# Causal mask of a cross attention: four products on TensorE, or a select on GpSimd

## What is computed

```
scores = jnp.einsum('bhqd,bhkd->bhqk', qh, kh) * inv_sqrt_d
causal = jnp.tril(jnp.ones((sq, sk), dtype=bool))
scores = jnp.where(causal, scores, jnp.finfo(scores.dtype).min)
attn = jax.nn.softmax(scores, axis=-1)
out = jnp.einsum('bhqk,bhkd->bhqd', attn, vh)
```

## Time and profile before

| | us |
|---|---|
| median of three runs | 1243.26 (1242.33 to 1248.41) |
| the profiled execution | 1251.86 |
| its span, first to last instruction | 1250.0 |

### The profile page before, as it was taken

One profiled execution on the slowest core, in us unless ns is written; L12 is line 12 of the kernel. 1 busy time (PEld: TensorE's weight loads), 2 busy tenths in 40 slices (PEclk: granted clock), 3 DMA queues, 4 the chain that ended last, 5 costly groups with the idle time before them and its releaser, 6 DMA issues. The chain is left out here.

```text
span 1250.0 us, 20961 instructions
## 1 busy us (share of the span) xinstructions
PE 1156.1 (92%) x7761; PEld 911.6 (73%) x7762; DVE 812.8 (65%) x1392; ACT 593.8 (48%) x1402; POOL 370.6 (30%) x279
## 2 busy tenths in 40 slices
PE   7989999999999999999999874899989999999992
PEld 3456677767776777677767653888779988889992
DVE  1155698789878988898889754532266666655660
ACT  1234554465445554555456422411156666656661
POOL 0011102212221222121212111401226566665662
PEclk9989999999999999999999895899989999989997
DMA  7910000000000000000000008202569999999964
GB/s 267 244 72 2 1 9 9 15 14 8 9 15 14 8 9 15 14 8 9 15 14 8 10 14 219 67 27 63 181 210 274 267 271 268 272 264 246 267 116 59
DMA packets 70459, 121.10 MB, mean 97 GB/s; under 512 B 18502, under 2 KB 22134, under 8 KB 70250
## 3 DMA queue, kind: packets, MB, share of 16 engines
q1 hardware_dynamic: 52682, 82.46, 20.4%
q0 software_dynamic: 17728, 37.97, 14.6%
HBM read 93.55 MB, written 28.13 MB: 97 GB/s over the span
## 5 line engine op out<-in xcount | busy, mean ns | idle before, releaser
L1323 POOL TENSOR_TENSOR rall<-qkv_var,phalf 100x17 f32<-100x17 f32 x16 | 49.2, 3074 | 415.4 <-DVE qkv_var L1046 415.4
L1389 POOL DMA_INDIRECT out_rows<-work,idx x64 | 127.9, 1998 | 113.4 <-issue 87.2
L375 PE MATMUL QS<-xh,wh 128*128 128x256 f32 x512 | 148.6, 290 | 0.0
L376 PE MATMUL QS<-xl,wh 128*128 128x256 f32 x512 | 146.0, 285 | 0.0
L377 PE MATMUL QS<-xh,wl 128*128 128x256 f32 x512 | 145.9, 285 | 0.0
L375 PE MATMUL W<-wch,oth 128*100 128x512 f32 x256 | 104.9, 410 | 0.0
L376 PE MATMUL W<-wcl,oth 128*100 128x512 f32 x256 | 100.7, 393 | 0.0
L377 PE MATMUL W<-wch,otl 128*100 128x512 f32 x256 | 100.4, 392 | 0.0
L376 PEld LDWEIGHTS QS<-xl,wh 128*128 128x128 f32 x512 | 99.4, 194 | 1.2
L375 PEld LDWEIGHTS QS<-xh,wh 128*128 128x128 f32 x512 | 99.4, 194 | 1.2
L377 PEld LDWEIGHTS QS<-xh,wl 128*128 128x128 f32 x512 | 99.2, 194 | 0.0
(11 more groups left out here) (206 smaller groups left out, 2874.8 us busy)
## 6 DMA issues: line engine op xcount, KB each, us to landing
raw<-in_w SPq DMA_DIRECT2D x24, 1024.0 KB
raw<-in_w SPq DMA_DIRECT2D x24, 512.0 KB
work<-in_w SPq DMA_DIRECT2D x8, 1024.0 KB
work<-in_w SPq DMA_DIRECT2D x8, 512.0 KB
hx_rows<-h3x SPq DMA_DIRECT2D x16, 212.5 KB
h_columns<-h3s SPq DMA_DIRECT2D x16, 200.0 KB, 1.9
h3T<-h_columns SPq DMA_DIRECT2D x16, 200.0 KB, 4.7
out_rows<-ytiles POOLq DMA_DIRECT2D x16, 200.0 KB, 2.5
```

The costliest lines, as they stand in the source:

```text
L375: mm(dst, ah, bh, start=start, stop=False)
L376: mm(dst, ah, bl, start=False, stop=False)
L1323: return nc.gpsimd.tensor_tensor(out=dst, in0=src, in1=phalf[:, 0:src.shape[1]], op=ALU.pow)
L1389: nc.gpsimd.indirect_dma_start(out, on_rows(idx[:, NE * j + e:NE * j + e + 1]), Y[e % 2][:, 512 * j:512 * (j + 1)], None, compute_op=ALU.a ...
```

## The change

The four products of line 490 are left out, and the first product of each bank in line 496 now opens the accumulation. ACT copies the unmasked scores to `PX` as before and raises `s.sx`. POOL then fills in the mask: one `affine_select` over the 16 heads of `PX`, in place, keeps an element where the query's number (the partition) less the key's number is 0 or more and writes -1e30 elsewhere, and raises `s.sx` a second time. It stands in POOL's queue between `ln1` and `qk`, behind a wait for ACT's copy. PE's queries wait for the copy alone; DVE's maximum in line 1106 waits for the select.

```diff
                     pe.wait_ge(s.ck, b)
-                    for j in range(4):
-                        mm(qb[j][0:T, 0:QW], identb[:, :], mask4[:, :], start=True, stop=False)
                     pe.wait_ge(s.qp, b)
                     for i in range(4):
                         for j in range(4):
 
                             r = slice(DX * j, DX * (j + 1))
                             last = mm(qb[j][0:T, T * i:T * (i + 1)], qpT[r, T * i:T * (i + 1)],
-                                      ckT[r, T * i:T * (i + 1)], start=False, stop=i == 3)
+                                      ckT[r, T * i:T * (i + 1)], start=i == 0, stop=True,
+                                      skip_group_check=True)
                     last.then_inc(s.sx_ps, 1)
...
                     if do.X:
-                        pe.wait_ge(s.sx, b)
+                        pe.wait_ge(s.sx, 2 * b - 1)
                     queries(b + 1)
...
                 if do.X:
-                    dve.wait_ge(s.sx, b)
+                    dve.wait_ge(s.sx, 2 * b)
                     red(mxx[:, :], X3, AX.X, ALU.max).then_inc(s.sx_max, 1)
...
                 if do.Q:
                     ln1(b + 1)
+                if do.X:
+
+                    wait_alone(pool, s.sx, 2 * b - 1)
+                    nc.gpsimd.affine_select(out=PX[0:T, :].rearrange("t (h n) -> t h n", n=T),
+                                            in_=PX[0:T, :].rearrange("t (h n) -> t h n", n=T), pattern=[[0, NX], [-1, T]],
+                                            compare_op=ALU.is_ge, fill=NEG, base=0, channel_multiplier=1).then_inc(s.sx, 1)
+                if do.Q:
                     qk(b + 1)
```

## The result

| | before | after |
|---|---|---|
| median of the runs | 1242.80 us (4 runs) | 1261.68 us (4 runs) |
| ratio, 95% interval | | 1.0158 (1.0084 to 1.0231) |
| profiled execution, its span | 1251.86, 1250.0 | 1268.49, 1266.2 |
| one step of the pipeline | 41.40 | 42.41 |
| last addition of line 1189 (b = 16) starts at | 766.95 | 783.82 |

The changed kernel is slower, by 19 us in the medians. The ratios leave out runs more than 1.5% above the fastest of the same kernel, and since the kernel before had single runs near 1230 us, that drops 9 of its 23 or 29 runs in the first eight experiments and at most 2 of the other kernel's, so there a ratio half a per cent above 1 decides nothing. The lines of the changed kernel are one less than before on DVE and ACT (1099 is 1098, 1106 is 1105, 1189 is 1188); the select is line 1343.

What follows compares the result with a forecast made beforehand. A loop of DVE up to the second `otl`, then PE, was taken to bound the step. 15 steps by 1.96 us plus 2.5 us in the last made 31.9 us, set on the median 1243.26: 1275 us, range 1244 to 1296.

Steps and rivals of the forecast that it cites:

- What bounds the step: Pipeline step of 41.40 us: DVE up to the second `otl`, then PE; removing PE's products gains nothing, at most 0.4 us.
- The start of the scores: Line 496 on PE: without the four products the scores can start some 0.4 us earlier, once `qpT` is copied.
- What the select disturbs: DVE lines 1099 and 1103, two SBUF operands each, and POOL's select run one after the other: 1.96 us a step.
- the first of the two ways: POOL first: line 1099 waits for the select's end, 1.96 us late; otherwise DVE goes on and line 1106 is 1.71 late.
- PE's waits: Transposes of line 515 would wait for `p_norm`; the `otl` wait at line 396 grows from 0.5 to some 2 us.
- The select's duration: POOL's select of 100 by 1600: 2.26 us from DVE's rate plus POOL's larger start; slow end 4.08 us.
- The sum: 15 steps by 1.96 us plus 2.5 us in the last, 31.9 us, set on the median: 1275 us.
- (a): Rival: engines run side by side, select hidden if at most 2.54 us; only the last step adds 2.5; 1246 us, chance 0.17.
- (b): Rival: side by side but a slow 4.08 us select, 1.54 us in each of 15 steps; 1271 us, chance 0.08.
- (c): Rival: select and DVE one after the other, and slow, 3.78 us by 15 and 4.3; 1304 us, chance 0.13.
- (d): Rival: PE closes the loop, select hidden; 15 by 0.4 us gained, 2.5 lost; 1240 us, chance 0.04.
- the point itself: Line 1106 on DVE: a select up to 2.54 us, DVE's other work, would be hidden if the engines do not disturb each other.

Runs made afterwards that it cites:

- The select aside: Kernel before, products kept, plus a POOL affine select of 100 by 1200 into its own tile, nobody waiting for it: step 42.05 us against 41.40, one run.
- the memset: Kernel before, products kept, plus a POOL memset of a bf16 100 by 1200 tile that nobody waits for: step 41.40 us, one run.
- the sums in PSUM: Changed kernel with the self-attention softmax's row sums and reciprocals in PSUM instead of SBUF: step 41.23 us, ratio to the kernel before 1.0017.
- the removal alone: Kernel before without the four products of line 490 and with no select, so unmasked: step 41.21 us, ratio 1.0059.
- the select behind the norm: Changed kernel with POOL's select waiting for DVE's product with the reciprocals (`p_norm`): step 44.85 us, every third or fourth 43.29, one run.

## Why the prediction was right, and what it mis-sized

**What bounds the step.** Right. PE at 92% was not the bound: taking its products away gave 0.19 us a step. I had said nothing, with 0.1 us at the second `otl`; that place was right and the size somewhat low. The start of the scores was put too early: I took 0.4 us, and it is 0.26, since PE takes up `qpT` only 0.15 us after its copy has ended (423.33 to 423.48 in the changed kernel). And DVE did not close the loop alone, as I had written: the kernel before was bounded by the second `oth`, with DVE 0.2 us ahead of it, so the first 0.2 us added to DVE cost nothing. Moreover the gain is not added to the loss. The select aside, with the products kept, lost 0.2 us less than the addition's delay, and the changed kernel, with the products gone, too (1.21 less 1.01): it is the same 0.2 us, by which `oth` came behind DVE, and either edit uses it up.

**What the select disturbs.** Right, and this was the step on which the forecast stood. Rows 11 had shown POOL waiting for DVE's instructions with two SBUF operands; the changed kernel shows the reverse order, DVE waiting for POOL, and the first of the two ways that I had weighed: the select starts 0.27 us before the addition, and the addition is held to the select's end. It shows as a longer addition, not as a later start as I had written. PE's waits came as the prediction had them, only shorter: 1.50 us for `otl` at line 396, with some 2 forecast, and a wait for `p_norm` at the transposes. Rows 12 stand beside this: the comparison with two SBUF operands was not held up 1.75 us after the start of a power of 17 columns, whereas selects of 1200 and 1600 columns held the addition until they had ended, give or take 0.04 us. What makes the difference (the prediction thought of operands that had been read by then) was not tested. The Trainium skill (SBUF — State Buffer, Who interferes with whom) states that a DVE instruction with two SBUF inputs contends with a GpSimd instruction that reads SBUF, and not with one that only writes it. The runs agree on both with 1.03 us beside the select and 0.17 us beside the memset.

**The select's duration.** The term that was mis-sized. I took 2.26 us, from DVE's pass and POOL's larger start; it is 1.64 us, and 1.27 us for 1200 columns. POOL's spans are rough, but its end is borne out by DVE, whose maximum starts 0.04 us behind it in the last step. The difference of 400 columns gives, as an estimate, 0.93 ns a column and about 0.16 us of start (the two forms differ in more than their length: the shorter one writes bf16). The 0.59 us of rows 9 are thus no start that every instruction of POOL has. The Trainium skill (GPSIMD Engine Reference, Performance pitfalls for Q7 kernels) has 1.03 cycles an element for an unrolled compare-and-select, 1.37 us here by its clock as an estimate; the run lies near that end of the range and not at its 2.03 cycles.

**The sum.** Forecast 1.96 us a step, measured 1.01. The select takes 0.62 less; the addition's own 0.17 us ran out with the select and was not made behind it; POOL picked the copy up after 0.23 and not 0.17 us, 0.06 more; 0.20 is the room at the second `otl`. 1.96 - 0.62 - 0.17 + 0.06 - 0.20 = 1.03. In the last step 2.5 us were forecast between the copy and the maximum and 1.87 measured, but the step grew by 0.2 us only. In all 15.1 us can be traced to the change, in place of 31.9. The median, 1261.68 us, lies 13 us below the 1275 forecast and inside the range. It is 18.9 us above that of the kernel before; some 4 us of this are not traced to the change, and that they fell on the forecast's side was luck.

**The rivals.** The engines side by side ((a) and (b)) is what the sums in PSUM make of the change: the select of 1.64 us is then hidden under DVE's 2.5 us of other work, as (a) has it, and only the condition that the engines do not disturb each other was not met. No run has a select near 2.54 us, so the point itself was not tested. (c) would have needed a slow select. (d) falls with the removal alone, which gave 0.19 us a step and not 0.4, and with the select's cost.

## What to carry to other kernels

Before giving POOL a pass over SBUF, list the DVE instructions that will run beside it and count their SBUF operands. Beside a select that reads SBUF, an addition with two was held until the select had ended, even over 16 columns, and the profile books it as busy time of the engine that is held. What ran beside POOL's work here without loss: instructions whose second operand lay in PSUM, and, beside a memset, which only writes, those with two SBUF operands too. And look for the wait that closes the loop before counting what a busy engine is spared: here four products on PE were worth 0.2 us a step, and one small addition on DVE was made 1.2 us longer.

## What the runs showed of the hardware that was not expected

- An addition of 100 by 16 took 1.39 us (1.19 to 1.52 in fifteen steps) in place of 0.17 beside POOL's select of 100 by 1600 (1.64 us), 1.03 us beside one of 100 by 1200 (1.27 us), 0.17 us beside a memset of 100 by 1200 (1.10 us), and 0.18 us beside the select when its sums lay in PSUM.
- With the select behind the norm, PE paused for 1.9 to 2.3 us ahead of line 396 in thirteen steps. In ten of them its granted clock then fell (1.00 to a mean of 0.66 to 0.69 over the next 5 us), with split products at 0.63 in place of 0.39 us and 1.56 us more in the step; in three the same pause cost nothing. Pauses of 0.9 us in the same place, in the middle steps of the changed kernel, were not followed by it.
- A product of DVE of 100 by 1600 with a broadcast operand of 100 by 16 takes the same 1.82 us from PSUM as from SBUF.
- The part behind the pipeline, which moves the experts' weights, took 467.8 to 484.1 us in the profiled executions, with as many instructions in all; the pipeline's middle steps mostly repeat to 0.02 us.
